# DLRM tower on one core: last one-hot table as a whole, two one-hots from the spread ids, first scores in columns, turned pairs and rows at other places

## The reference, cut to what matters

```python
e = jnp.stack([tbl_0[ids[:, 0]], ..., tbl_25[ids[:, 25]]], axis=1)   # 512 samples, 26 tables, 128 wide
T = jnp.concatenate([r_dense[:, None, :], e], axis=1)                # 27 features
Z = jnp.einsum('bnd,bmd->bnm', T, T)
z = Z[:, iu0, iu1]                                                   # 351 pairs above the diagonal
h = jnp.concatenate([z, r_dense], axis=1)
h = jnp.maximum(h @ W_top1 + b_top1, 0.0)                            # 479 x 512
h = jnp.maximum(h @ W_top2 + b_top2, 0.0)                            # 512 x 256
y = h @ W_top3                                                       # 256 x 1
```

## Time and profile before

| what | value |
|---|---|
| median of 3 runs | 116.38 us (116.02 to 116.89) |
| the profiled execution | 115.44 us |
| its span, first to last instruction | 113.6 us |
| TensorE busy | 106.1 us, 93% |
| VectorE busy | 91.0 us, 80% |
| ScalarE busy | 72.8 us, 64% |
| DMA traffic | 14.37 MB |

### The profile page before, as it was taken

One profiled execution on the slowest core, in us unless ns is written; L12 is line 12 of the kernel. 1 busy time (PEld: TensorE's weight loads), 2 busy tenths in 40 slices (PEclk: granted clock), 3 DMA queues, 4 the chain that ended last, 5 costly groups with the idle time before them and its releaser, 6 DMA issues.

```text
span 113.6 us, 2670 instructions
## 1 busy us (share of the span) xinstructions
PE 106.1 (93%) x997; PEld 88.9 (78%) x997; DVE 91.0 (80%) x224; ACT 72.8 (64%) x136; POOL 61.7 (54%) x59
## 2 busy tenths in 40 slices
PE   4999997999799999999999989996989999999992
PEld 4848675888577888888888989995889999978970
DVE  3598979999599999999999978986998269971230
ACT  5257665979978486685942777979956267461411
POOL 2778778777777787787877777777000000000000
PEclk9999999999999999999999999999999999999999
DMA  2897999999999959836355311121000000000000
GB/s 62 266 251 159 270 260 253 272 251 241 244 257 220 253 136 250 253 77 237 66 211 167 87 52 46 46 74 48 32 0 0 6 0 0 6 0 6 0 0 0
DMA packets 6592, 14.37 MB, mean 126 GB/s; under 512 B 2178, under 2 KB 3598, under 8 KB 6580
## 3 DMA queue, kind: packets, MB, share of 16 engines
q1 hardware_dynamic: 4772, 10.74, 36.4%
q0 software_dynamic: 1664, 3.41, 11.5%
q10 hardware_dynamic: 144, 0.05, 0.2%
HBM read 14.19 MB, written 0.02 MB: 125 GB/s over the span
## 4 chain that ended last, share of the span: by engine, by line
PE 67%; DMA 9%; ACT 8%; DVE 6%; issue 4%; SPq 3%; DVEq 0%
PE sums L629 17%; PE sums L631 17%; PE gram L674 10%; PE sums L714 5%; DMA raw<-tbl 5%; PE rowsT L652 4%; DMA ids_stored<-ids 4%; PE sums L719 3%; PE sums L640 2%; ACT table_h L417 2%; ACT featT L465 2%; PE rowsT L736 2%; PE mlpT L736 2%; PE sums L690 1%; DVE products L399 1%
## 5 line engine op out<-in xcount | busy, mean ns | idle before, releaser
L387 POOL DMA_INDIRECT rows<-tbl,idx_sb x52 | 60.9, 1172 | 17.0 <-PE sums L631 8.8
L629 PE MATMUL sums<-onehot,table_h 125*128 125x512 f32 (+1 forms) x116 | 45.6, 396 | 1.9 <-DVE onehot L516 1.8
L631 PE MATMUL sums<-onehot,table_l 125*128 125x512 f32 (+1 forms) x116 | 43.9, 382 | 0.0
L516 DVE TENSOR_SCALAR onehot<-ids_rel 125x512 fp32r<-125x512 f32 x118 | 42.1, 428 | 1.3 <-ACT ids_rel L430 1.3
L629 PEld LDWEIGHTS sums<-onehot,table_h 125*128 125x128 f32 x116 | 21.8, 188 | 7.9 <-DVE onehot L516 3.6
L631 PEld LDWEIGHTS sums<-onehot,table_l 125*128 125x128 f32 x116 | 21.9, 189 | 4.0 <-issue 0.2
L449 ACT COPY featT<-sums 128x512 f32<-128x512 f32 (+1 forms) x13 | 14.0, 1074 | 12.4 <-PE sums L631 12.4
L508 DVE TENSOR_TENSOR table_l<-raw,table_h 125x1280 fp32r<-125x1280 f32 (+2 forms) x13 | 17.4, 1340 | 2.5 <-ACT table_h L417 1.7
L417 ACT CAST table_h<-raw 125x1280 fp32r<-125x1280 f32 (+2 forms) x13 | 14.9, 1147 | 5.7 <-DMA raw<-tbl 5.7
L674 PE MATMUL gram<-featT 128*64 128x52 f32 x512 | 16.6, 222 | 0.3 <-ACT featT L465 0.3
L674 PEld LDWEIGHTS gram<-featT 128*64 128x64 f32 x512 | 15.6, 138 | 1.6 <-issue 1.2
(11 more groups left out here) (71 smaller groups left out, 101.5 us busy)
## 6 DMA issues: line engine op xcount, KB each, us to landing
raw<-tbl SPq DMA_DIRECT2D x7, 560.0 KB
raw<-tbl SPq DMA_DIRECT2D x5, 448.0 KB
raw<-w SPq DMA_DIRECT2D x3, 512.0 KB
ids_all<-ids_stored SPq DMA_DIRECT2D x10, 128.0 KB, 7.4
rows<-tbl,idx_sb POOLq DMA_INDIRECT x52, 5.6
raw<-tbl SPq DMA_DIRECT2D x7, 65.0 KB
raw<-tbl SPq DMA_DIRECT2D x1, 336.0 KB
raw<-tbl SPq DMA_DIRECT2D x5, 52.0 KB
```

The lines of the kernel that those rows point to most:

```text
L387: pool.indirect_dma_start(rows[:, t % 2, s, :], None, tables[f], bass.IndirectOffsetOnAxis(ap=idx_sb[:, t, f:f + 1], axis=0)).then_inc(row ...
L516: nc.vector.tensor_scalar(onehot[0:SELECT_PARTS, n % ONEHOTS, :], ids_rel[0:SELECT_PARTS, k % IDS_BUFFERS, :], float(c), None, ALU.is_equa ...
L629: nc.tensor.matmul(dst, table_h[0:SELECT_PARTS, n % PART_BUFFERS, c, :], hot, start=(c == 0), stop=False)
L631: nc.tensor.matmul(dst, table_l[0:SELECT_PARTS, n % PART_BUFFERS, c, :], hot, start=False, stop=(c == PLACES[n] - 1)).then_inc(chunk_selec ...
```

## The change

The last table is selected whole, all 512 samples for each place, in one bank. ScalarE copies samples 0 to 255 of it, then VectorE samples 256 to 511; the late steps are gone. `("weights_in", 0)` and `("dense_low", 0)` stand behind the first batch of products, `("weights_in", 1)` behind the second. `("pairsT", 0)` moves from behind P1[2] to behind pack 1, and the five later rows steps move, the last of them behind layer 1.

At the start TensorE spreads the ids of table 0 twice, into bank 3 and bank 0; those of tables 1 and 2 are spread between the products of the first places. VectorE builds the first two one-hots straight from bank 3. The second group of warm-up products is gone. `DIRECT` is 3, so the first raw transfer and the fp32 products take three places, and SyncE's wait at L347 is for three.

The scores of the first half become two columns of 128: four products with `h2T` as the weights and one column of `w3` moving, copied as 128x2, stored by a DMA of single elements.

```diff
 ...
 CHUNKS1 = PAIR_CHUNKS + 1
-WARM_UP_PRODUCTS = 3, 2
+WARM_UP_PRODUCTS = 3
+HEAD = 2
 ...
 LOADS = SELECTED_COUNT + WEIGHT_LOADS
-EARLY = 2 * P
-LATE_PARTS = 2
+ACT_SAMPLES = 2 * P
 ROWS_BEHIND = 2
-DIRECT = 2
+DIRECT = 3
 ...
     return min(12 * gather // 5 - 12, CHUNK0[-1])
-def late_places(part):
-    return range(PLACES[-1] * part // LATE_PARTS, PLACES[-1] * (part + 1) // LATE_PARTS)
 def schedule():
-    order = [("keep_warm", WARM_UP_PRODUCTS[0])] + [("spread_ids", k) for k in range(SPREAD_FIRST)]
-    order.append(("keep_warm", WARM_UP_PRODUCTS[1]))
+    order = [("keep_warm", WARM_UP_PRODUCTS), ("spread_ids", 0)]
 ...
     order += [
-        ("weights_in", 0), ("dense_low", 0),
-        ("select_late", 0), P0[0], row, ("weights_in", 1),
-        ("select_late", 1), P0[1], row,
-        P0[2], P0[3], ("pack", 0), P1[0], row,
-        P1[1], ("pack_act", 0), ("weights_in", 2), P1[2], ("pairsT", 0), row,
-        P1[3], ("pack", 1),
-        P2[0], ("pack_act", 1), P2[1], ("dense", 0), ("pairsT", 1), row,
-        P2[2], ("layer1", 0),
+        P0[0], ("weights_in", 0), ("dense_low", 0), row, P0[1], ("weights_in", 1), P0[2], row,
+        P0[3], ("pack", 0), P1[0], P1[1], row,
+        ("pack_act", 0), ("weights_in", 2), P1[2],
+        P1[3], ("pack", 1), ("pairsT", 0),
+        P2[0], ("pack_act", 1), P2[1], ("dense", 0), row, ("pairsT", 1),
+        P2[2], ("layer1", 0), row,
 ...
                              ).then_inc(b2_w3_landed, 16)
-            out_by_pair = out.rearrange("(t b) o -> t o b", b=SAMPLES)
-            for n in range(PAIRS):
-                sp.wait_ge(y_done, n + 1)
-                sp.dma_start(out_by_pair[n], y_row[:, SAMPLES * n:SAMPLES * (n + 1)]).then_inc(stored[n], 16)
+            sp.wait_ge(y_done, 1)
+            sp.dma_start(out[0:SAMPLES, :].rearrange("(t p) o -> p (t o)", p=P), y_col[:],
+                         allow_slow_non_contiguous=True).then_inc(stored[0], 16)
+            sp.wait_ge(y_done, 2)
+            sp.dma_start(out[SAMPLES:B, :].rearrange("b o -> o b"), y_row[:]).then_inc(stored[1], 16)
 ...
                 elif n == LOADS - 1:
-                    act.wait_ge(late_selected, PLACES[-1])
+                    act.wait_ge(chunk_selected, CHUNK0[-1])
 ...
                 if k < SPREAD_FIRST:
-                    act.wait_ge(ids_spread, k + 1)
+                    act.wait_ge(ids_spread, k + 2)
 ...
                     act.wait_ge(chunk_selected, CHUNK0[n + 1])
-                    samples = slice(0, B if n < SELECTED_COUNT - 1 else EARLY)
+                    samples = slice(0, B if n < SELECTED_COUNT - 1 else ACT_SAMPLES)
 ...
                                    ).then_inc(selected_copied, 1)
-                elif step == "select_late" and n == LATE_PARTS - 1:
-                    act.wait_ge(late_selected, PLACES[-1])
-                    nc.scalar.copy(slot_view(SELECT_SLOT0 + SELECTED_COUNT - 1, slice(EARLY, B)),
-                                   by_sample(sums[:, SELECTED_COUNT % 2, EARLY:B])).then_inc(late_copied, 1)
 ...
                     act.wait_ge(y_summed, n + 1)
-                    nc.scalar.copy(y_row[:, SAMPLES * n:SAMPLES * (n + 1)], score).then_inc(y_done, 1)
+                    nc.scalar.copy(*((y_col[:], score_col) if n == 0 else (y_row[:], score))).then_inc(y_done, 1)
 ...
                 if step == "select":
+                    if n == 0:
+                        dve.wait_ge(ids_spread, 1)
+                        dve.wait_ge(row0_ready, len(ROW0_AT))
+                        at = ROW0_AT[PLACES[0]]
+                        for c in range(HEAD):
+                            nc.vector.tensor_scalar(onehot[0:SELECT_PARTS, c, :], gram[0:SELECT_PARTS, SPREAD_FIRST, :],
+                                                    minus_row0[0:SELECT_PARTS, at:at + 1], float(c), ALU.add,
+                                                    ALU.is_equal).then_inc(onehot_built, 1)
 ...
                     middle = PLACES[n] // 2
-                    build_onehots(n, range(middle))
+                    build_onehots(n, range(HEAD if n == 0 else 0, middle))
 ...
                                          ).then_inc(padding_set, 1)
+                        dve.wait_ge(selected_copied, SELECTED_COUNT)
+                        samples = slice(ACT_SAMPLES, B)
+                        nc.vector.tensor_copy(slot_view(SELECT_SLOT0 + n, samples), by_sample(sums[:, n % 2, samples])
+                                              ).then_inc(last_copied_by_dve, 1)
 ...
                 return sums[:, u // BLOCKS, SAMPLES * (u % BLOCKS):SAMPLES * (u % BLOCKS + 1)]
+            def spread(table, bank):
+                nc.tensor.matmul(gram[:, bank, :], ones_at[:, table:table + 1].broadcast_to([P, P]),
+                                 ids_rows_r[:], start=True, stop=True).then_inc(ids_spread, 1)
 ...
                 elif step == "spread_ids":
-                    if n == 0:
-                        pe.wait_ge(ones_ready, 1)
-                        pe.wait_ge(ids_rows_ready, 1)
-                    nc.tensor.matmul(gram[:, n, :], ones_at[:, n:n + 1].broadcast_to([P, P]),
-                                     ids_rows_r[:], start=True, stop=True).then_inc(ids_spread, 1)
+                    pe.wait_ge(ones_ready, 1)
+                    pe.wait_ge(ids_rows_ready, 1)
+                    for bank in (SPREAD_FIRST, 0):
+                        spread(0, bank)
 ...
                         m = CHUNK0[n] + c
-                        samples = slice(0, B if n < SELECTED_COUNT - 1 else EARLY)
-                        dst, hot = sums[:, n % 2, samples], onehot[0:SELECT_PARTS, m % ONEHOTS, samples]
+                        dst, hot = sums[:, n % 2, :], onehot[0:SELECT_PARTS, m % ONEHOTS, :]
 ...
                             pe.wait_ge(load_low, 1)
+                        if 1 <= m < SPREAD_FIRST:
+                            spread(m, m)
 ...
                                              start=False, stop=(c == PLACES[n] - 1)).then_inc(chunk_selected, 1)
-                elif step == "select_late":
-                    if n == 0:
-                        pe.wait_ge(selected_copied, SELECTED_COUNT - 1)
-                    for c in late_places(n):
-                        hot = onehot[0:SELECT_PARTS, (CHUNK0[-2] + c) % ONEHOTS, EARLY:B]
-                        dst = sums[:, SELECTED_COUNT % 2, EARLY:B]
-                        for part in (table_h, table_l):
-                            last = nc.tensor.matmul(
-                                dst, part[0:SELECT_PARTS, (SELECTED_COUNT - 1) % PART_BUFFERS, c, :], hot,
-                                start=(c == 0 and part is table_h), stop=(c == PLACES[-1] - 1 and part is table_l))
-                        last.then_inc(late_selected, 1)
 ...
                         pe.wait_ge(ids_rel_done, SELECTED_COUNT)
-                    if n == BATCHES * EARLY // P:
-                        pe.wait_ge(late_copied, 1)
+                    if n == BATCHES * ACT_SAMPLES // P:
+                        pe.wait_ge(last_copied_by_dve, 1)
 ...
                         pe.wait_ge(dense_low, 1)
-                        pe.wait_ge(late_copied, 1)
+                        pe.wait_ge(selected_copied, SELECTED_COUNT)
+                        pe.wait_ge(last_copied_by_dve, 1)
 ...
                     pe.wait_ge(h2_by_act, n + 1)
-                    nc.tensor.matmul(score, b2_w3[:, 1, 0:1], h2T[:, 0, :], start=True, stop=False)
-                    pe.wait_ge(h2_by_dve, n + 1)
-                    nc.tensor.matmul(score, b2_w3[:, 1, 1:2], h2T[:, 1, :], start=False, stop=True
-                                     ).then_inc(y_summed, 1)
+                    if n == 0:
+                        pe.wait_ge(h2_by_dve, 1)
+                        for o in range(N2):
+                            for t in range(PAIR_TILES):
+                                last = nc.tensor.matmul(score_col[:, t:t + 1], h2T[:, o, P * t:P * (t + 1)],
+                                                        b2_w3[:, 1, o:o + 1], start=(o == 0 and t == 0),
+                                                        stop=(o == N2 - 1 and t == PAIR_TILES - 1))
+                        last.then_inc(y_summed, 1)
+                    else:
+                        nc.tensor.matmul(score, b2_w3[:, 1, 0:1], h2T[:, 0, :], start=True, stop=False)
+                        pe.wait_ge(h2_by_dve, n + 1)
+                        nc.tensor.matmul(score, b2_w3[:, 1, 1:2], h2T[:, 1, :], start=False, stop=True
+                                         ).then_inc(y_summed, 1)
```

More of the change, by code:

```diff
@@ L211, in build @@
         h2T = sb("h2T", [P, N2, SAMPLES])
-        y_row = sb("y_row", [1, B])
+        y_row = sb("y_row", [1, SAMPLES])
+        y_col = sb("y_col", [P, PAIR_TILES])
         sums = ctx.enter_context(nc.psum_tensor("sums", [P, 2, 512], fp32))
@@ L248, in build @@
         chunk_selected = sem("chunk_selected")
-        late_selected = sem("late_selected")
-        late_copied = sem("late_copied")
```

(4 more changed lines are left out.)

## The result

The changed kernel takes 119.39 us (median of 6), the kernel before 115.97 us (median of 6); the ratio is 1.0267, 95% interval 1.0202 to 1.0332: slower by 3.1 us. The profiled executions are 118.29 us (span 116.4) and 115.44 us (span 113.6), 2.85 apart.

The account below looks back on a forecast made before the run. TensorE and VectorE were taken to bound it together from 31.46 to 63.45 us, with ScalarE sharing the load from 68 to 83. Start +0.75, middle +1.8, scores -0.3 make +2.25 on 116.38: 118.6 us, range 116.3 to 120.3.

Parts of the forecast that it names:

- The weights behind P0[0] make VectorE late, and pairsT(1) with it: Middle: VectorE begins the first weights 3.55 us later, works 13.8 us unbroken, and pairsT(1) starts 1.6 us late.
- Layer 1 another 0 to 0.3 later, +1.8 in all: Behind pairsT(1): layer 1 starts 1.45 us late; the last group and P3[0]'s wait bring the middle to +1.8 us.
- ScalarE's cast behind the moved rows copy: Ahead of layer 1: ScalarE casts for it, 0.5 us, only after the moved rows copy, so layer 1 starts at 88.15.
- The clock in the middle: Around pairsT(1): no term for a fall of TensorE's clock; the clock was weighed only at the start.
- two microseconds of waiting ahead of pairsT(1): Middle: TensorE's earlier stalls of 0.68 and 0.46 us go and return as one wait of about 2 us there.
- First scores, -0.3: Kernel's scores: four column products in eight records take 0.5 us instead of 1.02, gaining 0.3 us, bounds 0 and 0.5.
- The start, +0.75: Kernel start: SyncE waits for three fp32 places, so table 3 is issued 0.75 us later, bounds 0 and 2.35.
- the DMA stage behind it is full and lands it later by the same amount: Start: table 3, issued 0.75 us later, also lands 0.75 us later, and every step up to 31.46 with it.
- the rise differs between runs of one kernel: Start: the moment TensorE reaches 2.4 GHz varies between runs, so the start costs anything from 0 to 2.35 us.
- The sum: Whole kernel: +0.75 + 1.8 - 0.3 = +2.25 us, giving a median of 118.6 us; chance 0.40.

Follow-up runs that it names:

- f4: The changed kernel with pairsT(0), pairsT(1) and the five rows steps at their old places: 118.35 us, 1.0172 of the kernel before.
- f2: The changed kernel with the first weights cast and split ahead of P0[0], second session: 118.05 us, 1.0102 of the kernel before.
- f3: The changed kernel with 14 products of unused result put into the wait ahead of pairsT(1): 117.98 us, 1.0093 of the kernel before.
- g2: The kernel before with the new start alone, first places in their own tile so SyncE has no wait: 1.0041 of the kernel before.
- g1: The kernel before with the new start alone, third session: 1.0070 of the kernel before.
- e2: The kernel before with the new start alone, first session: 1.0012 of the kernel before.
- f1: The changed kernel itself, measured again in the second session: 119.35 us, 1.0259 of the kernel before.
- e3: The kernel before with only the first scores in columns, first session: 1.0006 of the kernel before.
- e4: The changed kernel with the first weights cast and split ahead of P0[0], first session: 0.9967 of the kernel before.

## Why the prediction was right, point by point

- **The weights behind P0[0] make VectorE late, and pairsT(1) with it.** Right in size, and in mechanism as far as the chain shows it: 13.8 us of unbroken work were forecast, 71.61 to 85.50 is 13.9; VectorE started at 71.61 (72.1 forecast, less 0.3 of the start's shift), pairsT(1) came 1.54 us late (1.6), the wait was 2.09 (two). f4 shows that the order of the parts doesn't matter, only their sum. f2 shows that the cover isn't won back by moving the weights alone, since gathers and ScalarE's cast for w2 come next. How much of the lateness is the whole last table and how much the place of the weights is open.
- **Layer 1 another 0 to 0.3 later, +1.8 in all.** Without the fall of the clock layer 1 starts 1.45 us late (f3: 24.62 against 23.17): the forecast figure, but I had reached it by ScalarE's cast behind the moved rows copy. In f3 that cast is done at 90.22 and layer 1 starts at 90.36, right behind P2[2]; in the changed kernel the chain goes from P2[2] straight to layer 1. The cast was close, not the limit, and that the figure agrees is partly luck. In the changed kernel, with the fall, it is 2.39.
- **The clock in the middle.** Missing. I had written down "two microseconds of waiting ahead of pairsT(1)" and weighed the clock only at the start. The term that I put at nothing measures 1.5 us (f3; 51.29 - 49.81). What is left of middle and scores is 49.81 - 48.23 = 1.58 us, where I had 1.8 - 0.3 = 1.5.
- **First scores, -0.3.** Wrong: 0. My 0.5 us for eight records were 1.02, inside the bounds of 0.25 to 1.4. The nearer row was the turn of 128 columns, with as many weight columns; I had taken the pair products', with half as many.
- **The start, +0.75.** The step that failed is "the DMA stage behind it is full and lands it later by the same amount": the issue was 0.93 us later, the landing 0.43 earlier, and g2 moved the issue by 1.4 us for 0.1 us of landing. What the chain of f4 shows in its place is three slow places on TensorE that reach past the slack (argued, not tested). The size was in the bounds: 0.9 us in g1, none that shows in e2, -0.3 in the first trace. That the rise differs between runs of one kernel is borne out: the changed kernel issued table 3 at 9.79 in its first trace and at 10.86 in f1. Where exactly between 0 and 1 the cost lies is open.
- **The sum.** 2.25 us were forecast and 3.1 measured. The profiled execution adds up so: start -0.30 (forecast +0.75), middle and scores 1.58 (1.5), clock 1.48 (nothing), together 2.76. That the median lay 0.8 us from the forecast, and inside the range, is partly luck: a missing term of 1.5 us met a start that cost less in some executions than forecast, and the scores' missing 0.3 met a middle forecast 0.2 too long.

## What to carry to other kernels

A late step costs its own delay and can bring a stretch at 1.2 GHz behind the idle time that it makes; so price a new idle time twice, or fill or split it, as f3 and the old places did here (the splitting worked in three executions of four). When a step is moved out of another's shadow, add up the unbroken work of the engine that does it: the order inside the sum is free, the sum is not. And work for a later layer (w2) belongs in a wait that already exists, even when its data are there early.

## What the runs showed of the hardware that was not expected

TensorE's clock fell behind 2.09 us of idle time and stayed at the lower level for some 3.4 us (worked out from 0.55 over 2.5 us and 0.78 over 2.7), and what that costs depends on what runs there: 0.9 us in P2[2] and 0.5 in layer 1 in one trace, 0.2 and 1.2 in another.

In the first and third session every trace has a stretch of some 11 us, from about 70 to 82 us, in which TensorE again and again got one to five instructions and then stood for about 1.1 us, with nothing that it waited for. The kernel before was not traced there, but took 129.3 and 128.8 us as well. Here TensorE in e3, the kernel before with other scores:

```profile
78.24 0.37 PE L644 MATMUL sums<-onehot,table_l 125*128 125x256 f32 x1 [1.10 <-issue]
...
81.10 0.46 PE L678 MATMUL gram<-featT 128*64 128x52 f32 x3 [1.19 <-issue]
82.53 1.64 PE L678 MATMUL gram<-featT 128*64 128x52 f32 x26 [0.97 <-issue]
```

It is the place where many short products begin. What fed TensorE so slowly is not shown. From 66 to 84 us the queue that brings instructions moved one packet of 16 KB in e3 and three in the trace of before, which may be a consequence of the slow stretch as well as its cause. e4 and f2 are the same kernel on one chip, 129.13 and 118.05 us. Ratios from such a session can hide a loss: against the kernel before of its session that kernel reads 0.9967 (e4) and 1.0102 (f2).

A GpSimd gather, 0.94 to 1.99 us elsewhere in f2, took 3.25 (66.51 to 69.76) while VectorE did its memset and, right behind it, the subtractions of the first weights and of the dense features; the last of these ended at 69.55, 0.21 us before it. In e4, the same order, the gather ended at 72.12 and the subtraction at 71.91, 0.21 again. The memset alone does nothing of the kind: in the kernel before and in the changed one the gather that begins 0.82 us into it, as in f2, takes 0.94 us. And there, too, the gather beside the two subtractions ends 0.21 us behind the second: 68.96 to 70.61 against 70.40 before, 72.42 to 73.65 against 73.44 in the changed kernel. The Trainium skill (SBUF — State Buffer, "SBUF: two separate sides") says that VectorE can hold a pair of ports for a whole instruction, and that GpSimd can't write a DMA's descriptors until it lets go. The four endings agree with that; that the gather got no turn between two VectorE instructions in a row goes beyond it, and neither was tried by itself.
